# The first group's scores and row maxima in the last batch of the projection, in a three-layer transformer kernel

## What is computed

```python
x = x + self_attention(layernorm(x), w_qkv, w_out)              # causal, 16 heads of 32
x = x + cross_attention(layernorm(x), ctx, positions, ...)      # not causal, 32 heads of 16, axial rope
x = x + ffn_layer(layernorm(x), ...)                            # causal attention with rope (16 heads of 32), then a mixture of experts
# each attention:
scores = einsum('bqhd,bkhd->bhqk', q, k); attn = softmax(scores); out = einsum('bhqk,bkhd->bqhd', attn, v)
```

## Time and profile before

| | before |
|---|---|
| median of 3 runs | 2204.81 us (2203.09 to 2207.2) |
| the profiled execution | 2203.34 us, span 2201.6 us |
| mean granted TensorE clock | 0.959 |
| PE busy | 2027.0 us, 92% |
| PEld busy | 1360.0 us, 62% |
| DVE busy | 1210.9 us, 55% |
| ACT busy | 906.3 us, 41% |
| POOL busy | 694.9 us, 32% |

### The profile page before, as it was taken

The page is one execution under the profiler, slowest core; times in us unless marked ns, Lnnn a source line. Parts: engine busy times, 40 slices in busy tenths (PEclk is TensorE's granted clock), DMA queues, the critical chain, the costliest instruction groups (busy, mean ns, idle before and its releaser), DMA issues.

```text
span 2201.6 us, 31494 instructions
## 1 busy us (share of the span) xinstructions
PE 2027.0 (92%) x10679; PEld 1360.0 (62%) x10679; DVE 1210.9 (55%) x2649; ACT 906.3 (41%) x1699; POOL 694.9 (32%) x610
## 2 busy tenths in 40 slices
PE   7999999788699999996998999978999999999998
PEld 6876666566333333334776666657888887555554
DVE  6446666376689898875876666535323153121221
ACT  3435554355377676773443545434212221111111
POOL 0004655246323132322564755601000000233332
PEclk9997999999799999998997999989999999999999
DMA  5637766357654545444566766462111045233332
GB/s 196 221 155 161 167 159 134 112 191 264 210 138 119 148 110 148 100 126 120 191 211 202 167 152 154 112 219 96 43 54 60 18 179 222 56 65 62 62 61 37
DMA packets 150706, 297.15 MB, mean 135 GB/s; under 512 B 24530, under 2 KB 43092, under 8 KB 149524
## 3 DMA queue, kind: packets, MB, share of 16 engines
q1 hardware_dynamic: 112676, 241.64, 37.4%
q10 hardware_dynamic: 29136, 34.87, 6.0%
q0 software_dynamic: 8736, 18.62, 4.5%
HBM read 181.55 MB, written 102.50 MB: 129 GB/s over the span
## 4 chain that ended last, share of the span: by engine, by line
PE 43%; DVE 4%; DMA 3%; ACT 1%; issue 1%; POOL 1%; SPq 1%; ACTq 0%; POOLq 0%; DVEq 0%
PE bank L1702 10%; PE bank L1790 8%; PE bank L1713 5%; PE bank L1809 4%; PE bank L461 3%; PE bank L1083 2%; PE bank L1114 2%; PE bank L1155 2%; PE bank L1172 2%; DMA stack<-rotary_c_max_rows 1%; DMA normed<-xt 1%; PE bank L1123 1%; PE bank L1774 1%; PE bank L1117 1%; DVE rotary_p_hn L695 1%
## 5 line engine op out<-in xcount | busy, mean ns | idle before, releaser
L1275 ACT ACTIVATE cross_c_prob<-bank 128x512 f32<-128x512 f32 x512 | 271.0, 598 | 117.0 <-PE bank L1114 115.9
L1316 DVE TENSOR_REDUCE row_max<-bank 128x2 f32<-128x1024 f32 x256 | 299.7, 1212 | 27.4 <-PE bank L1083 26.4
L1702 PE MATMUL bank<-moe_hT,moe_w 128*128 128x512 f32 x1056 | 251.5, 394 | 10.1 <-DVE moe_prod L2075 5.5
L1083 PE MATMUL bank<-stack 48*128 48x512 f32 (+4 forms) x768 | 209.9, 454 | 39.8 <-PEq L71 24.4
L1114 PE MATMUL bank<-stack 56*128 56x512 f32 (+4 forms) x768 | 233.7, 429 | 13.1 <-DMA stack<-rotary_c_max_rows 5.3
L1702 PEld LDWEIGHTS bank<-moe_hT,moe_w 128*128 128x128 f32 x1056 | 199.8, 190 | 53.3 <-DVE moe_prod L2075 5.9
L1114 PEld LDWEIGHTS bank<-stack 56*128 56x128 f32 (+1 forms) x768 | 118.7, 193 | 144.1 <-ACT cross_c_prob L1275 68.9
L1790 PE MATMUL bank<-moe_w_e,moe_hT_e 128*128 x624 | 194.4, 465 | 4.4 <-DMA moe_w_e<-in_experts_packed 3.9
L1083 PEld LDWEIGHTS bank<-stack 48*128 48x128 f32 (+1 forms) x768 | 103.8, 201 | 121.0 <-DVE row_max L1316 50.3
L1790 PEld LDWEIGHTS bank<-moe_w_e,moe_hT_e 128*128 128x128 f32 x624 | 116.3, 191 | 66.1 <-issue 8.5
L1312 DVE CUSTOM_DVE_ANT_0 first_c_masked<-bank,later 128x128 f32<-128x128 f32 (+3 forms) x256 | 115.4, 485 | 71.2 <-PE bank L1083 70.3
(11 more groups left out here) (361 smaller groups left out, 4009.2 us busy)
## 6 DMA issues: line engine op xcount, KB each, us to landing
moe_w_e<-in_experts_packed SPq DMA_DIRECT2D x8, 2176.0 KB, 8.6
qk_parts<-first_p_parts SPq DMA_DIRECT2D x32, 512.0 KB, 2.8
stack<-qk_parts SPq DMA_DIRECT2D x64, 256.0 KB, 6.5
qk_parts<-cross_p_parts SPq DMA_DIRECT2D x32, 512.0 KB, 2.7
stack<-qk_parts SPq DMA_DIRECT2D x256, 64.0 KB, 2.5
qk_parts<-rotary_p_parts SPq DMA_DIRECT2D x32, 512.0 KB, 2.7
moe_raw<-in_shared_packed SPq DMA_DIRECT2D x11, 768.0 KB, 10.7
stack<-qk_parts SPq DMA_DIRECT2D x16, 512.0 KB, 5.2
```

The source lines that it names most:

```text
L1083: last = nc.tensor.matmul(bank[:, 0 : width_q(m)], q_stack[slot][r : r + PRODUCT_ROWS, at, m * P : (m + 1) * P], k_stack[slot][r : r + PRO ...
L1275: nc.scalar.activation(probability(g, step // HEADS_AT_ONCE, step % HEADS_AT_ONCE), psum[bank_at["score", n]][:, 0 : S - q0], ACT.Exp).the ...
L1316: nc.vector.tensor_reduce(row_max[:, g % 2, m, j - 1 : j + 1], c.banks[:, first : first + WIDE, :], AX_X, ALU.max).then_inc(s.max_done, 1)
L1702: last = nc.tensor.matmul(psum[bank][:], weights(pa, f, k), hT[p % 2][:, pb, k, :], start=m == 0, stop=m == len(steps) - 1)
```

## The change

In first, cross and rotary alike, the 16 score tiles of group 0 of batch 0 are issued by PE during the items 24 to 31 of the projection, two tiles behind each q or k product (`early_score`), into PSUM banks 0 to 2 (0 to 3 in cross). DVE takes their maxima at the end of each such item (`early_max`), behind shuffle, low and rotate. A score tile waits for the maximum that frees its bank. The core begins with group 1's lead tiles, and `split_max(0)` waits for no maximum.

The picking rows are written once per projection, by one ACT instruction behind item 8, into `raw0`, and SP sends them to the stacks: during the items 25 and 26 (25 to 28 in cross) for the stacks at hand, and for the stacks 2 and 3 of first and rotary in the core. In the core `send_max(0)` now stands ahead of `load_stack` for stack 2 on SP, and `take_max(0)` ahead of the DMAs of v on ACT. The three score banks of first and rotary are 0, 1, 2 in place of 0, 1, 4. Left out below: counters that are carried over, and changed semaphore values that follow from the above.

```diff
@@ -190,6 +190,8 @@
+        self.slots_at_hand = STACK_SLOTS if self.cross else 2
+        self.score_banks = 4 if self.cross else 3
         self.early_stacks = STACK_SLOTS - 1 if self.cross else 2
@@ -218,6 +220,20 @@
         send(a.k_stack, half, 2 * t.dh, 3 * t.dh, k[:, 1])
+def pick_rows(a):
+    return a.raw0[MAX_ROW:STACK_ROWS].rearrange("p (h n) -> p h n", h=HEADS_AT_ONCE)
+def load_picks(sp, a, slot, here):
+    t = Attention(a.kind)
+    for half in range(t.halves):
+        r = half * t.half_rows + 3 * t.dh
+        of_half = pick_rows(a).rearrange("p (h f) n -> p f h n", f=t.halves)[:, half]
+        sp.dma_start(a.k_stack[slot][r : r + 2 * HEADS_AT_ONCE].bitcast(F32), of_half).then_inc(here, 16)
@@ -337,8 +353,15 @@
         x_loaded = (s.x_loaded0, s.x_loaded1)
+        early_masked = hn[:, 0:2] if t.causal else None
+        stack_here = a.carried.stack_loaded0
+        def early_tiles(i):
+            return range(2 * (i - n_qk * (BODY - 1)), 2 * (i - n_qk * (BODY - 1)) + 2) if i >= n_qk * (BODY - 1) else ()
         SENDS, SENDS_AT_ONCE, FIRST_SEND_AT = SENDS_OF_STACK * t.halves, t.halves, 10
+        PICKS_AT = 25
@@ -390,6 +413,9 @@
                             n = bi * n_qk + 2 * m + (what == "k")
+                            if 0 <= n - PICKS_AT < t.slots_at_hand:
+                                sp.wait_ge(s.picks_made, 1)
+                                load_picks(sp, a, n - PICKS_AT, a.carried.picks_here)
                             at = (n - FIRST_SEND_AT) * SENDS_AT_ONCE
@@ -425,6 +451,18 @@
                         last.then_inc(s.transposed, 1)
+                    def early_score(n):
+                        m, j = divmod(n, HEADS_AT_ONCE)
+                        at, r = j // t.halves, j % t.halves * t.half_rows
+                        width = (m + 1) * P if t.causal else S
+                        if n == 0:
+                            pe.wait_ge(stack_here, 16 * (a.stacks_before + t.loads_of_stack))
+                        if n >= t.score_banks:
+                            pe.wait_ge(s.max_done, (n - t.score_banks) // t.halves + 1)
+                        nc.tensor.matmul(psum[n % t.score_banks][:, 0:width], a.q_stack[0][r : r + 3 * t.dh, at, m * P : (m + 1) * P],
+                                         a.k_stack[0][r : r + 3 * t.dh, at, 0:width], start=True, stop=True).then_inc(s.scores_ready, 1)
@@ -460,6 +498,9 @@
                         last.then_inc(s.proj_done, 1)
+                        if what in "qk":
+                            for tile in early_tiles(bi * n_qk + 2 * m + (what == "k")):
+                                early_score(tile)
                         if cross and what in "qk" and 2 * m + (what == "k") == TURN_CONTEXT_AT and bi + 1 < BODY:
@@ -592,6 +633,10 @@
                             nc.scalar.activation(parts[:, i % 2, 0], bank[:], ACT.Copy, scale=scale).then_inc(s.parts_hi, 1)
+                        if i == n_qk:
+                            act.wait_ge(s.lo_made, 3)
+                            nc.scalar.activation(pick_rows(a).bitcast(F32R), c.pick[MAX_ROW:STACK_ROWS, :].unsqueeze(2).to_broadcast([2 * HEADS_AT_ONCE, HEADS_AT_ONCE, S]),
+                                                 ACT.Copy).then_inc(s.picks_made, 1)
                         if bi + 1 < BODY:
@@ -736,6 +781,23 @@
                         nc.vector.tensor_tensor(parts[:, i % 2, 1], rotated_at(i), parts[:, i % 2, 0].bitcast(F32), ALU.subtract).then_inc(s.parts_lo, 1)
+                    def early_max(n):
+                        m, j = divmod(n, HEADS_AT_ONCE)
+                        if n % t.halves != t.halves - 1:
+                            return
+                        dve.wait_ge(s.scores_ready, n + 1)
+                        if t.causal:
+                            width = (m + 1) * P
+                            if n >= 2:
+                                dve.wait_ge(s.max_done, n - 1)
+                            nc.vector.tensor_tensor_reduce(out=early_masked[:, n % 2, 0:width], in0=psum[n % t.score_banks][:, 0:width], in1=c.later[:, S - width : S],
+                                                           scale=1.0, scalar=LOWEST, op0=ALU.add, op1=ALU.max,
+                                                           accum_out=a.row_max[:, 0, m, j : j + 1]).then_inc(s.max_done, 1)
+                        else:
+                            first = (n - 1) % t.score_banks
+                            nc.vector.tensor_reduce(a.row_max[:, 0, m, j - 1 : j + 1], c.banks[:, first : first + 2, :], AX_X, ALU.max).then_inc(s.max_done, 1)
@@ -791,6 +853,8 @@
                                                            parts[:, i % 2, 0].bitcast(F32), ALU.mult, ALU.subtract).then_inc(s.parts_lo, 1)
+                        for tile in early_tiles(i):
+                            early_max(tile)
                         if bi + 1 < BODY:
@@ -902,9 +965,12 @@
         VALUES_LAG, SUMS_STEP = 7 if cross else 9, 4
-        bank_score, bank_shared = ((0, 1, 2, 3), (4, 5, 7)) if cross else ((0, 1, 4), (2, 3, 7))
+        bank_score, bank_shared = ((0, 1, 2, 3), (4, 5, 7)) if cross else ((0, 1, 2), (3, 4, 7))
         bank_o, bank_sum = (6, 6) if cross else (5, 6)
         N_SCORE = len(bank_score)
+        EARLY = N16
+        tiles_made = lambda n: n - EARLY
+        maxima_made = lambda n: (n - EARLY) // WIDE
         bank_last = (0, 1, 2, 3)
@@ -1039,11 +1097,11 @@
                     wait_for_projection(sp, a)
+                    send_max(sp, 0)
                     for g in range(t.early_stacks, 3):
                         load_stack(sp, a, loop * BODY, g)
-                    if cross:
-                        load_picks(sp, 0)
-                    send_max(sp, 0)
+                    for slot in range(t.slots_at_hand, STACK_SLOTS):
+                        load_picks(sp, a, slot, s.picks_loaded)
                     for g in range(GROUPS):
@@ -1078,8 +1138,8 @@
                             pe.wait_ge(stack_loaded[slot], 16 * (a.stacks_before + t.loads_of_stack * (g // STACK_SLOTS + 1)))
-                        if n >= N_SCORE:
-                            pe.wait_ge(s.max_done, (n - N_SCORE) // WIDE + 1)
+                        if n >= N_SCORE + EARLY:
+                            pe.wait_ge(s.max_done, maxima_made(n - N_SCORE) + 1)
                         last = nc.tensor.matmul(bank[:, 0 : width_q(m)], q_stack[slot][r : r + PRODUCT_ROWS, at, m * P : (m + 1) * P],
@@ -1105,10 +1165,10 @@
                         if i == 0:
-                            if cross and g == 0:
-                                pe.wait_ge(s.picks_loaded, 16 * HALVES * STACK_SLOTS)
-                            if not cross and g < STACK_SLOTS:
-                                pe.wait_ge(s.picks_made, g + 1)
+                            if g == 0:
+                                pe.wait_ge(a.carried.picks_here, 16 * (a.picks_before + HALVES * t.slots_at_hand))
+                            if g == t.slots_at_hand:
+                                pe.wait_ge(s.picks_loaded, 16 * HALVES * (STACK_SLOTS - t.slots_at_hand))
                             pe.wait_ge(s.max_loaded, 16 * HALVES * (g + 1))
@@ -1195,8 +1255,6 @@
-                    for i in range(N16):
-                        scores(0, i)
                     for i in range(a.lead):
@@ -1243,21 +1301,11 @@
                     wait_for_projection(act, a)
+                    take_max(0)
                     for n in range(TT if cross else V_SLOTS - 1):
                         load_values(act, 0 if cross else n, n)
                     if cross:
                         act.dma_start(bo_row[:], a.bo.partition_broadcast(P)).then_inc(s.table_loaded, 16)
-                    if cross:
-                        nc.scalar.activation(pick_rows[MAX_ROW:STACK_ROWS], c.pick[MAX_ROW:STACK_ROWS, :].unsqueeze(2).to_broadcast([2 * HEADS_AT_ONCE, HEADS_AT_ONCE, S]),
-                                             ACT.Copy).then_inc(s.picks_made, 1)
-                        load_picks(act, 1)
-                    for slot in range(0 if cross else STACK_SLOTS):
-                        nc.scalar.activation(
-                            k_stack[slot][MAX_ROW:STACK_ROWS],
-                            c.pick[MAX_ROW:STACK_ROWS, :].unsqueeze(2).to_broadcast([2 * HEADS_AT_ONCE, HEADS_AT_ONCE, S]),
-                            ACT.Copy).then_inc(s.picks_made, 1)
-                    take_max(0)
                     for g in range(GROUPS):
@@ -1369,8 +1417,6 @@
                         wait_for_projection(dve, a)
-                    for i in range(N16):
-                        tile_max(0, i)
                     for i in range(a.lead):
@@ -1436,8 +1482,8 @@
-                        pool.wait_ge(s.max_done, N16 // WIDE * (g + 1))
                         if g:
+                            pool.wait_ge(s.max_done, maxima_made(N16 * (g + 1)))
                             pool.wait_ge(s.max_transposed, g)
...
```

(13 more changed lines are left out.)

11 lines of the change are left out of this document (6 added, 5 removed).

## The result

The changed kernel takes 2219.24 us (median of 5 runs, 2218.54 to 2225.36); beside it the kernel before took 2204.81 us (2200.33 to 2208.34, 5 runs). The ratio is 1.0070, with a 95% interval of 1.0055 to 1.0085: slower by some 14 us, where 7.8 us of gain were forecast. The profiled execution after took 2218.96 us (span 2217.2, mean granted clock 0.958), 15.6 us more than the one before.

The account below looks back on a forecast made before the run. PE, busy 92% of the span, was taken as the bound, with gain only at core starts: 22.4 - 4.4 - 1.2 - 5.3 - 3.4 - 0.3 = 7.8 us, giving 2197.0 us; range 2188.5 to 2204.

Parts of the forecast that it names:

- the rest of the span stays: Whole kernel: only the start of each core, ahead of its first score, can be shortened by the change.
- Part 1: Start of each core: maxima's DMA issued earlier by 6.7 us in first, 7.8 in cross, 7.9 in rotary; gain 22.4.
- The table load: ACT ahead of `take_max(0)`: a load of 1.28 us counted in each core, bounds 0 and 1.28.
- Part 2: Cores: stack 2 loaded later loses 4.4 us in first and rotary together; v beside the maxima in cross loses 1.2.
- The wait for stack 2: First score of group 2 in first and rotary: PE waits 2.2 us in each, bounds 0 and 4.
- rival (a): Table load (+3.8 us) or late stack 2 (+4.4) stays hidden: about 2193 us, both 2189; chance 0.28.
- the low end: Cross: maxima land late beside v's loads by 0 to 4.7 us; 1.2 taken, as SP issues no later than ACT.
- Part 3: Scores moved into the projection lose 5.3 us in first, 3.4 in rotary and 0.3 in cross.
- PE's wait for DVE behind the angles: Last batch of first: PE waits 1.9 us for the maximum of tile 8, bounds 0.5 and 3.
- Rival (c): Cross and rotary projections: maxima exceed the DVE and POOL loop's idle time, 15.4 us more, 2212.4 us; chance 0.08.

Follow-up runs that it names:

- The swap alone: Kernel before, with only `send_max(0)` put ahead of `load_stack` on SP and no work moved into the projection: 2216.94 us, ratio 1.0072.
- the filled gap: Changed kernel with 24 extra matmuls on PE in each causal phase where it waits for group 1's maxima: 2211.34 us, ratio 1.0038.

## Why the prediction was wrong

**What bounds it.** Right as far as it went: the head of each core was the place, and it became shorter. Wrong was "the rest of the span stays": the head was also the time in which stack 2 and v came in. From the 7.8 us of gain to the 15.6 of loss are 23.4 us. The causal cores make 21.3 of them (25.7 lost where 4.4 were forecast), the heads of cross and rotary 3.7 and 0.7, what stands behind the last core 1.1; the projections give back 2.9 and the core of cross 0.5.

**Part 1, the gain.** Right in first and rotary. In first the maxima's DMA is issued 3.81 us behind the first score (forecast 3.65); in rotary it is 4.8 and in cross 5.0, where PE also waits, 0.9 and 0.8 us, for POOL's split ahead of the transposes. The heads of first and rotary lose 6.7 and 7.2 us (forecast 6.7 and 7.9). The table load stood where the earlier trace rows had put it, 1.28 us with the copy 0.02 us behind it.

**Part 2, the step that failed.** The wait for stack 2 was sized well, 2.2 and 2.0 us, forecast 2.2 each. But the prediction followed the moved transfers only to their own reader. It bounded their cost at 0 to 4 us in each causal phase; measured are 13.3 and 12.4. In first these are 2.2 for stack 2, 8.0 for group 1's maxima, and 3.1 left over, of which some 2 are the clock by the filled gap; in rotary 2.0, 4.3 and 6.1, of which about 5. The last two terms, group 1's maxima and the clock, the sum put at nothing and gave no reason. What it left out: `send_max(1)` stands on ACT's queue behind `wo`'s 1 MB, and both share the engines with stacks 2 and 3. The window that showed a DMA share of 1.08 until 177 us was read for when stack 2 ends; it said as well that full engines were being moved to where the next deadline is. (They were full for some 8 us there, from 169 to 177 us, not the 9 that rival (a) speaks of: over the first 1.2 us the share was 0.03.) The swap alone, in the kernel before, makes the time as long (1.0072), and undoing it brings the causal cores back to 235.5 and 234.8 us.

In cross the maxima landed 4.5 us later than before (8.7 instead of 4.24), forecast 1.2 with bounds 0 to 4.7: the term was inside its bounds, at their upper end, and the head is 2.9 us shorter, not the 6 without which the prediction called itself wrong. The reason given for the low end, that SP issues first, was wrong: ACT issues v's loads while its table is loaded, 1.9 us ahead of SP:

```profile
595.67 1.31 ACTq L1057 DMA_DIRECT2D cross_c_v<-values  x3
...
597.58 1.45 SPq L1077 DMA_DIRECT2D stack<-cross_c_max_rows  x2
...
606.31 0.80 PE L1174 MATMUL bank<-stack 56*128 56x512 f32 x2 [5.71 <-DMA stack<-cross_c_max_rows]
```

**Part 3, the projection.** First: +6.5 us, forecast 5.3 (bounds to 6.4), with PE's wait for DVE behind the angles at 1.8 us as derived from the earlier trace rows (forecast 1.9):

```profile
PE bank L464 <- DVE row_max L795: 1.8, 1, 1.8
```

Rotary: +1.4, forecast 3.4; cross: -1.8, forecast +0.3. Together 6.1 instead of 9.0. In first and cross that is one trace each: the second trace of the changed kernel has +4.4 and +0.4, and with +1.2 in rotary the same 6.0. Rival (c), maxima that don't fit into the loop of DVE and POOL, did not happen: in cross a rotate still comes every 3.5 us, with DVE idle for 0.41 us ahead of it.

**The rivals.** None was what came. The outcome was slower, to which I gave 0.08, and through another mechanism than the one priced for it, so those 0.08 are no credit. The range ended at 2204 with 4 us for each causal phase in part 2; the 13.3 and 12.4 in their place are 17.7 more, which is past the measured time. So it was this one bound that failed.

**What was worth doing.** With the transfers in their old order the kernel gains nothing (1.0016), as the maxima of the causal phases then land behind stack 2; cross, whose stacks 0 to 2 are sent during the projection, keeps some 3 us by the traces. The times of the kernels that keep only this, or this and one thing more (0.9981 to 1.0004), are too close to 1 to confirm it by themselves.

## What to carry to other kernels

When a change shortens a stretch, list the transfers that were hidden in it and ask whose deadline they meet next; a full DMA share in the old stretch is a debt, not a free resource. Price a transfer put behind a wait not by its own reader alone but by every small transfer issued while it runs, here 64 KB that took 13 us instead of 6 or less. And add to each new wait of PE of several us what the lower clock costs behind it.

## What the runs showed of the hardware

Times are from issue to PE's use. 64 KB of maxima took 3.3 us with a DMA share of 0.74 meanwhile; 13.3 us with a share of 1.09 and 1 MB ahead on the queue; and 6.1 us or less with the same 1 MB ahead and a share of 0.53. On a queue of their own, beside stack 2 (1.5 MB) and then stack 3 on the other, they took 9.8 us, no less than the 9.6 us behind stack 2 on the same queue. After 8.0 us without matmuls the clock was 0.52 over the next 8.8 us; with 24 useless matmuls in a gap of 6.9 us it was 1.00 throughout, and the next 8.9 us held 65 matmuls where at 0.52 8.5 us held 32. An engine's DMA issue overtook its own table load: the loads of v were issued at 595.67, while ACT's table load ran from 595.61 for 1.28 us and the copy ahead of them in the program began at 596.90. First shows the same (175.16, 175.10 and 176.40).
